# Order of the attention scores in layer 1, and of the passage from layer 0, in a four-layer graph kernel

## Chip, cores and metric

The kernel runs on one core of a Trainium2 chip. The metric is the device time of one execution in microseconds; lower is better. The engines of a core have instruction queues of their own and meet only at semaphores: PE (matrix products, which end in PSUM banks), DVE and ACT (elementwise work, reading PSUM and SBUF), POOL (elementwise work on SBUF), SP (issues DMA transfers here).

## What is computed

64 graphs of 128 nodes with 256 features pass four layers; each is followed by a residual and a layer norm, `x = layernorm(x + layer(x, adj))`. The change touches layer 0 at its end and layer 1. Layer 0 applies hypergraph convolution, relu, layer norm, hypergraph convolution. Layer 1 is, cut to its core:

```python
q, k = split(x @ W_qk.T)                # 64 columns each
v = x @ W_v.T
scores = (q @ k.T) / 8
w = sum(scores * adj, axis=-1)          # one number a node
w = softmax(w, over the nodes)
out = w * v
```

Since only the sum over the neighbours is needed, w(n) is q(n) times the sum of adj(n, m) k(m): one product of the adjacency matrix with k, then a row sum.

## The kernel before

Four graphs make a group; there are G = 16 groups. Each layer is written for each engine as a `step(g, p, has)`, which holds that engine's work of one step in a fixed order, for groups around g; `has(k)` is true when group g + k exists. `over_layers` runs all steps of one layer and then those of the next. At a passage between two layers a string (`SEAMS_ACT`, `SEAMS_POOL` and so on, one string a passage) says in which order the last steps of the old layer (o) and the first of the new one (n) are written. So the order on each engine is written by hand; no scheduler changes it.

Products are made in three float16 passes (`triple`, lines 86 to 88: low times high, high times low, high times high). For this every group of x is split into a high and a low half of float16 (tiles x_halves): ACT makes the high half (`x_high`, line 1123; for the first two groups of layer 1 `first_high`, line 720), POOL the low half (`x_low`, line 1130; `first_low`, line 967), and SP has both transposed by DMA (tiles xT_hi, xT_lo, line 1144; line 514 for the first two). Group g and g + 2 share one pair of buffers.

Layer 1, one step on each engine, in order:

- PE: `project(g - 1, 3)`, the fourth graph's product with W_qk and W_v of the group before (6 matmuls a graph); `weight_columns(g - 2)` (line 1236), which turns the softmax weights wn back to columns; `project(g, 0)`; `aggregate(g - 1)` (line 1224), adjacency times k, four graphs; `project(g, 1)` and one half of `project(g, 2)`; `score_rows(g - 1)` (line 1232), which turns the scores w to rows; the other half of `project(g, 2)`.
- ACT: `high_half(g + 3)`; `norms(g - 2)`, the four norm applies that write x_resident (line 1078); `copy_qkv(g + 1, 0)`, the first graph's v, q, k from PSUM to the tile l_vqk (line 1281); `exponentials(g)` (l_wexp, line 1293); the copies of graphs 1 to 3.
- DVE: the residuals l_pre of g - 2 (line 1327), `scores(g - 1)` (l_qa line 1341, l_w line 1348), two norm rows, `minimum(g - 1)` (l_wmin, line 1354), two norm rows, `softmax(g - 1)` (l_wrec line 1358, l_wn line 1362), and the norm's variance (ends in l_veps, line 1058).
- POOL: `norm_scales(g - 2)` (l_msum, l_mneg, l_rstd line 1069, l_nmr line 1072), then the low half of group g + 3.

Each engine runs on its own count of steps: the exponential of a group comes before its softmax, that before its weight columns, these before its residuals.

The end of layer 0: PE projects the hidden features h with W2 graph by graph (`project(g, j)`; graph j needs that zf of graph j - 2 is copied), ends with `square_sums` (line 616) and makes the last product in `mix_z` (line 629) out of zn. ACT copies zf (`copy_z`, line 702) and makes `squares_high` (hqs_hi, line 696); POOL adds the squares hq (line 973), makes `squares_low` (hqs_lo, line 980) and raises the variance to the power -1/2 (`hidden_power`, zrs, line 963); DVE makes zn (line 886), the low half of h (h_lo, line 839), and the counts rcs. In ACT's step G - 1 both `first_high` stand behind the last square of group G - 1 and ahead of the norm applies of G - 3 and of `copy_z(G - 1, 0)`. On POOL all of layer 0 is written before anything of layer 1.

Of the kernel before, what the change touches and what calls it, by code (L numbers as in the profile page):

```python
# [14 lines left out]
G = GRAPHS // GP  # L15
# [8 lines left out]
SEAMS_ACT = ('nnnonn', 'nononono', 'ooonnnonn')  # L24
SEAMS_DVE = ('oononn', 'onono', 'nonn')
SEAMS_POOL = ('ooooo', 'onno', 'ooonnn')
# [410 lines left out]
def layer0(nc, K, ctx, tiles, weights):  # L437
# [21 lines left out]
    L = norm(nc, ctx, "l0", 2, tiles)  # L459
# [209 lines left out]
    def scalar(act):  # L669
# [47 lines left out]
        def first_high(g):  # L717
            act.wait_ge(px_ps, upto(G - 2 + g, 2, 2))
            act.wait_ge(L.x_new, upto(g, GP, GP))
            act.activation(K.F.xs[g][0], x_group(K, g), ACT.Copy).then_inc(K.F.x_hi, 1)  # L720
# [8 lines left out]
        def step(g, p, has):  # L729
# [6 lines left out]
            if has(-1):  # L736
                copy_z(g - 1, 1)
                copy_z(g - 1, 2)
# [8 lines left out]
            if has(-1):  # L747
                copy_z(g - 1, 3)
            if has(0):
                hidden(g, 0)  # L750
                hidden(g, 1)
                square(g, 0)
# [14 lines left out]
            if isinstance(g, int) and g == G - 1:  # L767
                first_high(0)
                first_high(1)
            if has(-2):  # L770
                norm_apply(K, L, act, g - 2, p, 0)
                norm_apply(K, L, act, g - 2, p, 1)
                norm_apply(K, L, act, g - 2, p, 2)
                norm_apply(K, L, act, g - 2, p, 3)
            if has(0):
                copy_z(g, 0)
                squares_high(g)
# [171 lines left out]
    def gpsimd(pool):  # L949
# [32 lines left out]
        def step(g, p, has):  # L982
            q = 1 - p
            if isinstance(g, int) and g == G - 2:
                first_low(0)
                first_low(1)
# [4 lines left out]
            if has(0):  # L991
                norm_scales(K, L, pool, g, p)
            if has(1):
                hidden_power(g + 1)
            if has(2):
                sum_squares(g + 2, 1)
# [10 lines left out]
        return step, 2, 0  # L1007
# [140 lines left out]
def layer1(nc, K, ctx, tiles):  # L1148
# [41 lines left out]
    def tensor(pe):  # L1190
        def project(g, p, j, half=None):
            if j == 0:
                transposed(F, pe, g, p)
# [45 lines left out]
        def step(g, p, has):  # L1239
# [5 lines left out]
            if has(0):  # L1245
                project(g, p, 0)
            if has(-1) and g < G:
                aggregate(g - 1, q)
            if has(0):
                project(g, p, 1)  # L1250
                project(g, p, 2, 0)
            if has(-1) and g < G:
                score_rows(g - 1, q)
            if has(0):
                project(g, p, 2, 1)
# [10 lines left out]
    def scalar(act):  # L1266
# [29 lines left out]
        def step(g, p, has):  # L1296
# [5 lines left out]
            if has(1):  # L1302
                copy_qkv(g + 1, q, 0)
            if has(0) and g < G - 1:
                exponentials(g, p)
            if has(1):
                copy_qkv(g + 1, q, 1)
                copy_qkv(g + 1, q, 2)
# [761 lines left out]
```

## Time and profile before

| | |
|---|---|
| runs, median (lowest to highest) | 676.03 us (675.19 to 676.68), 3 runs |
| profiled execution | 676.46 us, span of its instructions 674.7 us |
| PE busy | 622.4 us, 92% of the span |
| DVE busy | 564.2 us, 84% |
| ACT busy | 525.5 us, 78% |
| POOL busy | 378.5 us, 56% |
| DMA | 76.14 MB, mean 113 GB/s |

Layer 0 lasts until about 290 us, layer 1 until about 387, layers 2 and 3 fill the rest. A busy share is a mean over all of it; what a reordering is worth is read from the stretches in which PE stands. A line of the timeline has the start, the duration, the engine, line and operation, the output and the inputs, and in square brackets the idle time of the engine ahead of it and what ended it. Durations of matmuls overlap.

### The profile page before, as it was taken

Reading aid. Unit: us, or ns where it says so; the run is one execution under the profiler, and the core shown is the slowest. Engines: PE = TensorE matmul, PEld = TensorE weight load, DVE = VectorE, ACT = ScalarE, POOL = GpSimd, SP = SyncE. Lnnn points to the kernel's source line nnn. Section 1 sums busy time; section 2 is a strip of 40 time slices with the busy share of each in tenths; the row PEclk is TensorE's granted clock in tenths of the full one; section 3 lists DMA queues with packets and bytes.
Section 4 is the critical chain, followed back from the end, with each engine's and each line's share of the span. In section 5 each row is a group of like instructions: output and inputs, shape, how many; then the busy total and the mean of one; then the engine's idle time right before and its main releaser. Section 6 shows DMA issues by size and latency. Waiting matters only on the chain.

```text
span 674.7 us, 15857 instructions
## 1 busy us (share of the span) xinstructions
PE 622.4 (92%) x5014; PEld 451.5 (67%) x5014; DVE 564.2 (84%) x1712; ACT 525.5 (78%) x1191; POOL 378.5 (56%) x448
## 2 busy tenths in 40 slices
PE   5889999999999999779999979999999996999993
PEld 4567777777777776556666647665766663788882
DVE  3889998888888886769999889898988987588886
ACT  4667888877777777767888777787877885799995
POOL 1335556665555555746777434443435353799983
PEclk9999999999999999989999999999999999999998
DMA  9781439464636322544665334445454443477883
GB/s 272 185 223 48 83 65 229 83 149 86 146 83 165 78 33 32 93 95 83 92 95 107 65 64 94 97 93 96 94 102 88 102 88 64 80 182 187 185 185 126
DMA packets 174467, 76.14 MB, mean 113 GB/s; under 512 B 122161, under 2 KB 173873, under 8 KB 174385
## 3 DMA queue, kind: packets, MB, share of 16 engines
q1 hardware_dynamic: 164208, 66.34, 42.9%
q0 software_dynamic: 8448, 8.39, 8.6%
q8 instruction: 41, 0.67, 0.4%
q10 hardware_dynamic: 1728, 0.40, 0.3%
q14 instruction: 42, 0.34, 0.2%
HBM read 28.97 MB, written 8.39 MB: 55 GB/s over the span
## 4 chain that ended last, share of the span: by engine, by line
PE 26%; POOL 9%; DVE 8%; ACT 6%; DMA 5%; issue 4%; ACTq 0%; POOLq 0%; SPq 0%; DVEq 0%
PE banks L86 8%; PE banks L88 8%; PE banks L87 8%; POOL l_rstd L1069 4%; DMA xT_lo<-x_halves 3%; ACT x_resident L1078 3%; POOL x_halves L1130 3%; DVE l_st L1044 2%; DMA l_TT_lo<-l_T_lo 2%; POOL l_U L2036 2%; PE banks L1593 1%; ACT l_wexp L1293 1%; DVE l_wn L1362 1%; DVE l_pre L2005 1%; DVE l_veps L1058 1%
## 5 line engine op out<-in xcount | busy, mean ns | idle before, releaser
L1078 ACT ACTIVATE x_resident<-l_pre,l_nmr,l_rstd 128x256 f32<-128x256 f32 x256 | 140.7, 605 | 15.6 <-POOL l_nmr L1072 15.6
L973 POOL TENSOR_TENSOR hq<-hq 128x512 f32<-128x512 f32 x48 | 69.5, 1448 | 93.7 <-ACT hq L690 91.4
L1130 POOL TENSOR_TENSOR x_halves<-x_resident,x_halves 128x1024 f16<-128x1024 f32 x46 | 98.1, 2134 | 3.9 <-ACT x_halves L1123 3.2
L1044 DVE BATCH_NORM_STATS2 l_st<-l_pre 128x6 f32<-128x256 f32 x256 | 93.4, 410 | 0.0
L86 PE MATMUL banks<-Wk_lo,xT_hi 128*128 128x512 f16 (+1 forms) x256 | 83.5, 326 | 3.2 <-DVE l_pre L1327 1.8
L1069 POOL TENSOR_TENSOR l_rstd<-l_veps,minus_half 128x4 f32<-128x4 f32 x64 | 74.9, 1170 | 17.9 <-DVE l_veps L1058 14.2
L87 PE MATMUL banks<-Wk_hi,xT_lo 128*128 128x512 f16 (+1 forms) x256 | 83.3, 325 | 0.0
L88 PE MATMUL banks<-Wk_hi,xT_hi 128*128 128x512 f16 (+1 forms) x256 | 83.2, 325 | 0.0
L86 PE MATMUL banks<-W2T_lo,h_hi 128*128 128x257 f16 x256 | 70.3, 274 | 5.3 <-ACT zf L702 4.4
L88 PE MATMUL banks<-W2T_hi,h_hi 128*128 128x257 f16 x256 | 70.1, 274 | 0.0
L87 PE MATMUL banks<-W2T_hi,h_lo 128*128 128x257 f16 x256 | 70.1, 274 | 0.0
L677 ACT ACTIVATE hf<-banks,b_col 128x512 f32<-128x512 f32 x64 | 44.5, 696 | 26.9 <-PE banks L88 26.8
L839 DVE TENSOR_TENSOR h_lo<-hf,h_hi 128x512 f16<-128x512 f32 x64 | 42.8, 690 | 12.1 <-issue 8.2
L1833 POOL TENSOR_TENSOR l_T_lo<-l_tf,l_T_hi 128x512 f16<-128x512 f32 x16 | 18.5, 1158 | 58.7 <-ACT l_T_hi L1684 58.7
L1063 POOL TENSOR_TENSOR l_msum<-l_st 128x4 f32<-128x4 f32 x64 | 13.6, 213 | 66.7 <-DVE l_st L1044 66.2
L86 PE MATMUL banks<-xT_lo,W1T_hi 128*128 128x512 f16 x128 | 48.6, 379 | 1.8 <-DVE xT_lo L853 1.1
L1123 ACT ACTIVATE x_halves<-x_resident 128x1024 f16<-128x1024 f32 x46 | 48.4, 1052 | 1.9 <-DMA xT_lo<-x_halves 1.9
L88 PE MATMUL banks<-xT_hi,W1T_hi 128*128 128x512 f16 x128 | 48.5, 379 | 0.0
L87 PE MATMUL banks<-xT_hi,W1T_lo 128*128 128x512 f16 x128 | 48.5, 379 | 0.0
L86 PE MATMUL banks<-w_lo,xT_hi 128*128 128x1 f16 (+1 forms) x256 | 45.5, 221 | 3.2 <-ACT l_xw L1934 1.9
L87 PE MATMUL banks<-w_hi,xT_lo 128*128 128x1 f16 (+1 forms) x256 | 46.5, 220 | 0.0
L88 PE MATMUL banks<-w_hi,xT_hi 128*128 128x1 f16 (+1 forms) x256 | 46.5, 221 | 0.0
(200 smaller groups left out, 1933.7 us busy)
## 6 DMA issues: line engine op xcount, KB each, us to landing
adj<-in_adj SPq DMA_DIRECT2D x32, 256.0 KB, 3.4
x_halves<-in_x SPq DMA_DIRECT2D x16, 512.0 KB, 4.4
x_resident<-b_half SPq DMA_DIRECT2D x8, 1024.0 KB, 7.1
x_resident<-in_x POOLq DMA_DIRECT2D x16, 512.0 KB, 6.0
out<-x_resident SPq DMA_DIRECT2D x15, 512.0 KB, 3.2
x_resident<-in_L_gnn_W SPq DMA_DIRECT2D x2, 512.0 KB, 5.5
x_resident<-in_L_gnn_Wk SPq DMA_DIRECT2D x1, 768.0 KB, 9.4
xT_hi<-x_halves SPq DMA_TRANSPOSE x48, 3.2
```

The source lines that it names most:

```text
L86: nc.tensor.matmul(out, lhs[0], rhs[1], start=start, stop=False, **kw)
L87: nc.tensor.matmul(out, lhs[1], rhs[0], start=False, stop=False, **kw)
L88: return nc.tensor.matmul(out, lhs[0], rhs[0], start=False, stop=stop, **kw)
L677: act.activation(hf[:, h, :], b_hid[h % 2][:], ACT.Relu, bias=K.b1[:, h:h + 1], scale=1.0 / W_SCALE).then_inc(hf_ok, 1)
L839: dve.tensor_tensor(hs[1][:, h, :], hf[:, h, :], hs[0][:, h, :], ALU.subtract).then_inc(h_lo, 1)
L973: pool.tensor_tensor(hq[:, 0, :], hq[:, 0, :], hq[:, h, :], ALU.add).then_inc(hqs_ok, 1)
L1044: dve.bn_stats(L.st[p][:, j, :], L.pre[p][:, j, :]).then_inc(L.st_ok, 1)
L1069: pool.tensor_tensor(L.rstd[p][:], L.veps[p][:], K.minus_half[:], ALU.pow).then_inc(L.rstd_ok, 1)
L1078: act.activation(K.x[:, gcols(g, j)], L.pre[p][:, j, :], ACT.Identity, bias=L.nmr[p][:, j:j + 1], scale=L.rstd[p][:, j:j + 1]).then_inc(L. ...
L1123: act.activation(F.xs[p][0], x_group(K, g), ACT.Copy).then_inc(F.x_hi, 1)
L1130: pool.tensor_tensor(F.xs[p][1], x_group(K, g), F.xs[p][0], ALU.subtract).then_inc(F.x_lo, 1)
L1833: pool.tensor_tensor(ts[1][:], tf[:], ts[0][:], ALU.subtract).then_inc(t_lo, 1)
```

## The change

It has two parts. In layer 1 PE makes `project(g, 0)` in two halves with `aggregate(g - 1)` between them, then `project(g, 1)`, then `score_rows(g - 1)`, then all of `project(g, 2)`; and ACT makes `exponentials(g)` ahead of `copy_qkv(g + 1, 0)`. At the passage from layer 0 the `first_high` move to ACT's steps G - 2 and G - 1, the `first_low` to POOL's steps G - 4 and G - 3, the zf copies of the last group are set between the norm applies of group G - 3, the last norm scales go behind `hidden_power` of the last group, and the low halves of groups 2 and 3 (layer 1) ahead of the norm scales of group G - 1.

```diff
 
 SEAMS_SP = ('noonnn', 'oono', 'onooonon')
 SEAMS_PE = ('nonn', 'onononono', 'oon')
-SEAMS_ACT = ('nnnonn', 'nononono', 'ooonnnonn')
+SEAMS_ACT = ('nnononn', 'nononono', 'ooonnnonn')
 SEAMS_DVE = ('oononn', 'onono', 'nonn')
-SEAMS_POOL = ('ooooo', 'onno', 'ooonnn')
+SEAMS_POOL = ('nonno', 'onno', 'ooonnn')
 
 W_SCALE = 64.0
 SQ_SCALE = 0.5
@@ -733,7 +733,7 @@
                 mixed_high(g, p, 1)
             once(g, -2, W.vectors, act)
             once(g, 0, W.high_w2, act)
-            if has(-1):
+            if has(-1) and g < G:
                 copy_z(g - 1, 1)
                 copy_z(g - 1, 2)
             once(g, 1, W.high_qkv, act)
@@ -744,8 +744,12 @@
             once(g, 4, W.high_w3, act)
             once(g, 5, W.high_wk, act, 0)
             once(g, 6, W.high_wk, act, 1)
-            if has(-1):
+            if g == G - 2:
+                first_high(0)
+            if has(-1) and g < G:
                 copy_z(g - 1, 3)
+            if g == G - 1:
+                first_high(1)
             if has(0):
                 hidden(g, 0)
                 hidden(g, 1)
@@ -764,15 +768,21 @@
             once(g, -1, W.halve_b2, act)
             if has(2):
                 copy_adj(g + 2)
-            if isinstance(g, int) and g == G - 1:
-                first_high(0)
-                first_high(1)
+            if g == G - 1:
+                copy_z(G - 1, 0)
             if has(-2):
                 norm_apply(K, L, act, g - 2, p, 0)
                 norm_apply(K, L, act, g - 2, p, 1)
+            if g == G - 1:
+                copy_z(G - 1, 1)
+            if has(-2):
                 norm_apply(K, L, act, g - 2, p, 2)
                 norm_apply(K, L, act, g - 2, p, 3)
-            if has(0):
+            if g == G - 1:
+                copy_z(G - 1, 2)
+                squares_high(G - 1)
+                copy_z(G - 1, 3)
+            if has(0) and g < G - 1:
                 copy_z(g, 0)
                 squares_high(g)
         return step, 2, 2
@@ -981,17 +991,20 @@
 
         def step(g, p, has):
             q = 1 - p
-            if isinstance(g, int) and g == G - 2:
-                first_low(0)
-                first_low(1)
             once(g, -2, W.constants, pool)
             once(g, -2, W.sum_rows, pool)
             if has(1):
                 squares_low(g + 1)
-            if has(0):
+            if has(0) and g < G - 2:
                 norm_scales(K, L, pool, g, p)
             if has(1):
                 hidden_power(g + 1)
+            if g > G - 2:
+                norm_scales(K, L, pool, g - 1, 1 - p)
+            if g == G - 4:
+                first_low(0)
+            if g == G - 3:
+                first_low(1)
             if has(2):
                 sum_squares(g + 2, 1)
             if has(0):
@@ -1004,7 +1017,7 @@
             once(g, 2, W.low_w3, pool)
             once(g, 3, W.low_wk, pool, 0)
             once(g, 4, W.low_wk, pool, 1)
-        return step, 2, 0
+        return step, 2, 1
 
     return sync, tensor, scalar, vector, gpsimd
 
@@ -1189,7 +1202,7 @@
 
     def tensor(pe):
         def project(g, p, j, half=None):
-            if j == 0:
+            if j == 0 and half != 1:
                 transposed(F, pe, g, p)
             if half == 1:
                 pass
@@ -1243,16 +1256,16 @@
             if has(-2) and g <= G:
                 weight_columns(g - 2, p)
             if has(0):
-                project(g, p, 0)
+                project(g, p, 0, 0)
             if has(-1) and g < G:
                 aggregate(g - 1, q)
             if has(0):
+                project(g, p, 0, 1)
                 project(g, p, 1)
-                project(g, p, 2, 0)
             if has(-1) and g < G:
                 score_rows(g - 1, q)
             if has(0):
-                project(g, p, 2, 1)
+                project(g, p, 2)
             if g == G + 1:
                 project(G - 1, 1, 3)
             if g == G + 2:
@@ -1299,11 +1312,10 @@
                 high_half(g + 3, q)
             if has(-2) and g < G - 1:
                 norms(g - 2, p)
-            if has(1):
-                copy_qkv(g + 1, q, 0)
             if has(0) and g < G - 1:
                 exponentials(g, p)
             if has(1):
+                copy_qkv(g + 1, q, 0)
                 copy_qkv(g + 1, q, 1)
                 copy_qkv(g + 1, q, 2)
             if has(1) and g < G - 2:
```

PE, one step in the steady part of layer 1, before (tiles named with their buffer numbers; l1_wn0 the weights of one group, l1_vqk1 the k of the next, xT0 the halves of the one behind it):

```order
L1236 MATMUL banks<-ident,l1_wn0 128x4
L86 MATMUL banks<-qkvT_lo,xT0_hi 128x384
L87 MATMUL banks<-qkvT_hi,xT0_lo 128x384
L88 MATMUL banks<-qkvT_hi,xT0_hi 128x384
L86 MATMUL banks<-qkvT_lo,xT0_hi 128x384
L87 MATMUL banks<-qkvT_hi,xT0_lo 128x384
L88 MATMUL banks<-qkvT_hi,xT0_hi 128x384
L1224 MATMUL banks<-l1_vqk1,adjT_resident 128x65 x4
```

and now:

```order
L1249 MATMUL banks<-ident,l1_wn0 128x4
L86 MATMUL banks<-qkvT_lo,xT0_hi 128x384
L87 MATMUL banks<-qkvT_hi,xT0_lo 128x384
L88 MATMUL banks<-qkvT_hi,xT0_hi 128x384
L1237 MATMUL banks<-l1_vqk1,adjT_resident 128x65 x4
L86 MATMUL banks<-qkvT_lo,xT0_hi 128x384
```

The adjacency products moved up by three matmuls; the matrix product that turns the scores to rows (with l1_w) now stands 12 matmuls behind the one with l1_wn0, not 15.

ACT, one step in the steady part of layer 1, before (x1_halves is the high half three groups on, l1_vqk1 v, q, k of one group, l1_wexp0 the exponential of the group before it):

```order
L1123 ACTIVATE x1_halves<-x_resident 128x1024
L1078 ACTIVATE x_resident<-l1_pre0,l1_nmr0,l1_rstd0 128x256 x4
L1281 ACTIVATE l1_vqk1<-banks 128x384
L1293 ACTIVATE l1_wexp0,l1_wsum0<-banks,l1_wmin0 4x128
L1281 ACTIVATE l1_vqk1<-banks 128x384 x3
L1123 ACTIVATE x0_halves<-x_resident 128x1024
```

and now:

```order
L1136 ACTIVATE x1_halves<-x_resident 128x1024
L1091 ACTIVATE x_resident<-l1_pre0,l1_nmr0,l1_rstd0 128x256 x4
L1306 ACTIVATE l1_wexp0,l1_wsum0<-banks,l1_wmin0 4x128
L1294 ACTIVATE l1_vqk1<-banks 128x384 x4
L1136 ACTIVATE x0_halves<-x_resident 128x1024
```

The exponential stands ahead of all four copies; the rest is as it was.

POOL, the end of layer 0, before, from the zrs of group G - 2 to that of G - 1 (x0_halves and x1_halves are the low halves of groups 0 and 1 of layer 1):

```order
L963 TENSOR_TENSOR zrs<-zvar,minus_half 128x4
L973 TENSOR_TENSOR hq<-hq 128x512
L952 DMA x_resident<-in_x 128x4x256
L973 TENSOR_TENSOR hq<-hq 128x512 x2
L967 TENSOR_TENSOR x0_halves<-x_resident,x0_halves 128x1024
L967 TENSOR_TENSOR x1_halves<-x_resident,x1_halves 128x1024
L980 TENSOR_TENSOR hqs_lo<-hq,hqs_hi 128x512
L1063 TENSOR_TENSOR l0_msum<-l0_st0 128x4
L1065 TENSOR_TENSOR l0_mneg<-l0_msum,minus_half 128x4
L1069 TENSOR_TENSOR l0_rstd0<-l0_veps0,minus_half 128x4
L1072 TENSOR_TENSOR l0_nmr0<-l0_mneg,l0_rstd0 128x4
L963 TENSOR_TENSOR zrs<-zvar,minus_half 128x4
```

and now, from the same zrs on:

```order
L973 TENSOR_TENSOR zrs<-zvar,minus_half 128x4
L977 TENSOR_TENSOR x1_halves<-x_resident,x1_halves 128x1024
L983 TENSOR_TENSOR hq<-hq 128x512
L962 DMA x_resident<-in_x 128x4x256
L983 TENSOR_TENSOR hq<-hq 128x512 x2
L990 TENSOR_TENSOR hqs_lo<-hq,hqs_hi 128x512
L973 TENSOR_TENSOR zrs<-zvar,minus_half 128x4
L1076 TENSOR_TENSOR l0_msum<-l0_st0 128x4
L1078 TENSOR_TENSOR l0_mneg<-l0_msum,minus_half 128x4
L1082 TENSOR_TENSOR l0_rstd0<-l0_veps0,minus_half 128x4
L1085 TENSOR_TENSOR l0_nmr0<-l0_mneg,l0_rstd0 128x4
L1143 TENSOR_TENSOR x0_halves<-x_resident,x0_halves 128x1024
```

The low half of group 0 went one step further up (behind the zrs of group G - 3), that of group 1 directly behind this zrs; the zrs of the last group stands ahead of the norm scales of group G - 2, and behind these follows the low half of group 2 (the last row), which stood behind the norm scales of group G - 1 before.

## Rows read from the trace of the kernel before

**Rows 1.** stages; columns: window, its length, busy (x count) by engine, PEclk, DMA share, GB/s

```profile
277.00:299.75 22.75, 14.95 (x106) 10.15 (x104) 17.23 (x36) 14.29 (x30) 15.33 (x16) 1.00 0.59 102
299.75:303.00 3.25, 3.25 (x13) 2.39 (x14) 0.00 (x0) 1.55 (x2) 2.02 (x1) 0.50 0.98 250
308.51:375.35 66.84, 64.34 (x424) 42.80 (x423) 60.69 (x217) 58.53 (x133) 49.28 (x61) 1.00 0.58 97
```

**Rows 2.** timeline of ACT, one period of layer 1

```profile
330.77 2.08 ACT L1078 ACTIVATE x_resident<-l_pre,l_nmr,l_rstd 128x256 f32<-128x256 f32 x4 [0.69 <-POOL l_nmr L1072]
332.75 0.47 ACT L1281 ACTIVATE l_vqk<-banks 128x384 f32<-128x384 f32 x1
333.12 0.34 ACT L1293 ACTIVATE l_wexp<-banks,l_wmin 4x128 f32<-4x128 f32 x1
...
333.46 1.21 ACT L1281 ACTIVATE l_vqk<-banks 128x384 f32<-128x384 f32 x3
...
336.34 2.08 ACT L1078 ACTIVATE x_resident<-l_pre,l_nmr,l_rstd 128x256 f32<-128x256 f32 x4 [0.72 <-POOL l_nmr L1072]
```

**Rows 3.** timeline of DVE, the same period

```profile
330.90 0.42 DVE L1341 SCALAR_TENSOR_TENSOR l_qa<-banks,l_vqk 128x256 f32<-128x256 f32 x1 [0.23 <-PE banks L1224]
...
332.48 0.28 DVE L1354 TENSOR_REDUCE l_wmin<-banks 4x1 f32<-4x128 f32 x1
...
333.59 0.15 DVE L1358 RECIPROCAL l_wrec<-l_wsum 4x1 f32<-4x1 f32 x1 [0.18 <-ACT l_wexp L1293]
...
334.56 1.69 DVE L1327 SCALAR_TENSOR_TENSOR l_pre<-l_vqk,banks,x_resident 128x256 f32<-128x256 f32 x4
```

**Rows 4.** timeline of POOL, the same period

```profile
334.62 1.29 POOL L1069 TENSOR_TENSOR l_rstd<-l_veps,minus_half 128x4 f32<-128x4 f32 x1 [0.61 <-DVE l_veps L1058]
...
336.32 2.13 POOL L1130 TENSOR_TENSOR x_halves<-x_resident,x_halves 128x1024 f16<-128x1024 f32 x1
```

**Rows 5.** timeline of PE, one period, four of its rows

```profile
334.14 0.38 PE L1236 MATMUL banks<-ident,l_wn 4*128 4x4 f32 x2 [0.24 <-DVE l_wn L1362]
...
335.44 1.00 PE L1224 MATMUL banks<-l_vqk,adjT_resident 128*128 128x65 f32 x8
336.27 0.33 PE L86 MATMUL banks<-qkvT_lo,xT_hi 128*128 128x384 f16 x1
...
337.74 0.27 PE L1232 MATMUL banks<-ident,l_w 128*4 128x128 f32 x1
```

**Rows 6.** timeline of PE, the passage from layer 0

```profile
280.22 0.28 PE L86 MATMUL banks<-W2T_lo,h_hi 128*128 128x257 f16 x1 [2.55 <-ACT zf L702]
...
284.30 0.16 PE L616 MATMUL banks<-ones,hqs_lo 128*128 128x1 f16 x1 [1.25 <-issue]
...
299.75 0.50 PE L86 MATMUL banks<-qkvT_lo,xT_hi 128*128 128x384 f16 x1 [3.55 <-DMA xT_lo<-x_halves]
```

**Rows 7.** timeline of POOL, the passage

```profile
278.87 4.21 POOL L967 TENSOR_TENSOR x_halves<-x_resident,x_halves 128x1024 f16<-128x1024 f32 x2
...
293.57 4.21 POOL L1130 TENSOR_TENSOR x_halves<-x_resident,x_halves 128x1024 f16<-128x1024 f32 x2
```

**Rows 8.** chain of waits, the passage: start, us, what

```profile
295.72 3.99 DMA xT_lo<-x_halves
```

**Rows 9.** timeline of DVE, the passage

```profile
269.38 1.67 DVE L886 SCALAR_TENSOR_TENSOR zn<-zf,zrs,W2beta_rows 128x256 f32<-128x256 f32 x4 [1.13 <-POOL zrs L963]
...
294.94 0.83 DVE L1362 TENSOR_SCALAR l_wn<-l_wexp,l_wrec 4x128 f32<-4x128 f32 x1
296.24 3.01 DVE L1327 SCALAR_TENSOR_TENSOR l_pre<-l_vqk,banks,x_resident 128x256 f32<-128x256 f32 x4 [0.47 <-PE banks L1236]
```

**Rows 10.** timeline of ACT, end of layer 0 and first norm apply of layer 1

```profile
251.17 0.39 ACT L702 ACTIVATE zf<-banks 128x257 f32<-128x257 f32 x1 [1.31 <-PE banks L88]
...
268.76 0.69 ACT L677 ACTIVATE hf<-banks,b_col 128x512 f32<-128x512 f32 x1 [1.11 <-PE banks L88]
...
308.51 2.08 ACT L1078 ACTIVATE x_resident<-l_pre,l_nmr,l_rstd 128x256 f32<-128x256 f32 x4 [0.67 <-POOL l_nmr L1072]
```

## Prediction

> **What bounds the kernel now.** I read the page first, then the windows by stage, then the timeline of each engine over one period of layer 1, and last the timeline of the passage from layer 0. The page gives PE 92% of the span, so a change that only reorders work can win only where PE stands still or waits in a loop with the others. Two such places lie where the change works.
>
> *Layer 1 in its steady part.* From 308.51 to 375.35 us layer 1 takes twelve equal periods of 5.57 us; a twelfth of the busy times is PE 5.36, DVE 5.06, ACT 4.88 us, at granted clock 1.00 [rows 1]. None is full, so I looked for a loop. It is there in the rows, with starts counted from x_resident on ACT at 330.77: the four norm applies until the copy at 332.75 (1.98), that copy (0.37), the exponential until the reciprocal on DVE at 333.59 (0.47), wn and the variance until rstd on POOL at 334.62 (1.03), rstd and nmr until the next x_resident at 336.34 (1.72) [rows 2 to 4]. The sum is 5.57, the whole period. PE waits in it: 0.24 us ahead of the weight columns at 334.14 [rows 5]. The matmul ends are modelled: one lasts 0.33 but the next starts 0.163 later (nine between 336.27 and 337.74 [rows 5]), so PE is really free some 0.17 earlier and needs 5.57 - 0.41 = 5.16 us a period. DVE waits 0.23 (for the adjacency products) and 0.18 (for the exponential) [rows 3]: it needs 5.16 too.
>
> *The passage.* Between 277.00 and 299.75 PE is busy 14.95 of 22.75 us [rows 1]. Its three large waits: 2.55 us for zf, which ACT copies only after two x_halves and four norm applies; 1.25 us for the squares, which stand on POOL behind 4.21 us of x_halves; 3.55 us for the transposed halves of group 2 [rows 6, 7]. Those came late because POOL made x_halves at 293.57, behind norm scales, and the transposition followed at 295.72 and took 3.99 [rows 7, 8]. After that wait PE runs 3.25 us at granted clock 0.50, the 1.2 GHz level, where it was 1.00, the 2.4 GHz level, before the wait [rows 1]; the 2.55 us wait didn't bring it down.
>
> **The change, steady part.** No instruction is added or dropped in the period. On ACT the exponential moves ahead of the first copy of v,q,k, so the copy's 0.37 us leaves the loop: 5.57 - 0.37 = 5.20. The copy itself costs nothing there: its reader is PE's project(g+2, 0) behind the weight columns, 0.5 us or more away, and the fourth copy keeps its place since the two only change places. The condition is that the minimum is ready at 332.75. It ends at 332.48 + 0.28 = 332.76 [rows 3], a tie; the PE edit makes room: the products come three matmuls earlier (3 x 0.163 = 0.49 us), of which DVE can use its 0.23 us wait, and the turned scores come 12 matmuls behind the weight columns and not 15, so they are not late for the minimum.
>
> The PE edit has a price. The products wait for the fourth copy, which ends at 333.46 + 1.21 = 334.67; they start at 335.44 [rows 2, 5], 0.77 later. Now they come 0.49 earlier by order and up to 0.37 earlier with wn: 0.09 too early, and with some 0.15 from release to first matmul they start 0.2 to 0.25 later than PE could. Following it round: products at x_resident + 4.10; 5.16 - 0.31 - 0.49 = 4.36 on, the weight columns; 0.42 on, l_pre; 1.68 on, qa; 1.58 on, the minimum, which ends 2.02 behind the next x_resident (ready 2.08), against 1.98 wanted. That adds up to 0.1 to one round, and settled over several rounds the period is 5.25 us; bounds 5.20 (the ACT loop alone) and 5.57 (nothing gained). A loss has no row for it except the rival below. I take 5.25, since every term but the 0.15 is read: 12 x 0.32 = **3.8 us gained**.
>
> **The change, passage.** *Price.* The first two low halves on POOL (4.21 us for two [rows 7]) move two and one steps up, each right behind zrs. For the second the rows show what stands beside it: the same zrs releases DVE's zn x4 at 269.38 [rows 9]. While POOL works on x_halves (from 293.57, two of 2.1 us [rows 7]) some DVE operations wait: wn at 294.94 lasts 0.83 and ends at 295.77, as the first of the two ends, and l_pre x4, begun at 296.24 inside the second, takes 3.01 against 1.69 in the steady part [rows 3, 9]. zn, too, has two inputs in SBUF. So zn comes 2.1 us later. PE's mix_z waits 0.9 for it, and the fourth h_lo behind it is late for the W2 projection: 1.0 to 1.1 us lost. One step up the same happens to rcs_lo and zn: 1.1 more. Together 2.1; bounds 0 and 4.2. The high halves on ACT (about 1.0 us each) fall into its waits for PE of 1.31 us ahead of zf and 1.11 ahead of hf [rows 10], and cost nothing; without that cover it would be 1.0 each.
> The Trainium skill (SBUF — State Buffer, "SBUF: two separate sides") says that POOL and a DVE operation with two SBUF inputs share one pair of ports and the first holds it for its whole instruction; by that rule the trace agrees for x_halves.
>
> *Gain.* ACT copies zf(0) right after the last squares, so the 2.55 goes; POOL goes to the squares' low half without the 4.21, and its next limit is ACT's high half behind the third zf copy. Counted with the 2.1 of shift: last W2 projections end 282.4, square sums 283.3 instead of 284.30. zrs now stands ahead of the norm scales: zn at 285.2, mix_z at 286.5, 1.1 earlier. Then POOL makes the low half of group 2 at 287.1 to 289.2 (now 293.57), SP issues its transposition right behind the high one, at 290.7 instead of 295.72, landing at 294.7. PE is then held by wn of group 0: ACT reaches that exponential at 293.0 (norm apply waits for the fourth copy now), and wn runs into the low half of group 3 on POOL, until 295.1. project(2) starts at 295.7 instead of 299.75, at full clock. One period on, wn of group 1 runs into the low half of group 4 (POOL 300.1 to 302.3), so weight columns at 302.6, rstd 303.0, first x_resident of the steady part at **304.7 instead of 308.51** [rows 10]: **3.8 us gained**, the price already in it. Bounds: 1.7 if the two stalls cost all of 4.2, 7.5 if neither they nor the wn collisions come (2.1 + 1.6 more).
>
> Behind layer 1 nothing is touched; the shift is carried on, since PE, DVE and ACT go on in order. Adjacency loads for layer 2 stand long before their use.
>
> **The sum** is made against the profiled execution's 676.46 us (span 674.7): 676.46 - 3.8 - 3.8 = 668.9. The median of the runs is 0.43 lower, 676.03; so 668.4.
>
> **Rivals.** (a) *The loop gains nothing.* PE, waiting for the fourth copy, is late with the weight columns, and DVE with the minimum, by as much as ACT wins. For it: three engines need 5.16 to 5.20, a tie. Against: 0.25 us of wait is less than the 0.41 PE has. Time 676.0 - 3.8 = 672.2.
> (b) *The passage gains nothing.* The port stalls in layer 0 and the two at wn eat it. For: four stalls of up to 2.1 us. Against: 3.55 us and the half clock behind it fall away. Time 676.0 - 3.8 = 672.2.
> (c) *Slower: POOL takes the ports ahead of the fourth l_pre in each period.* Now l_pre x4 starts at 334.56, its fourth at 335.8, and x_halves on POOL at 336.32 [rows 3, 4]: 0.5 us of room. It decides from there: if the weight columns are more than 0.5 late behind wn, the fourth l_pre waits 2.1 us, and with it products, minimum and exponential: some 1.8 a period. The period behind it, PE is early again, so I count every second: 6 x 1.8 = 11 lost against 7.6 gained, 679.4; every period would be 690. Against it: I find PE 0.1 to 0.2 late, not 0.5.
> The same page's rule would have rstd, if it started first, hold the ports for its whole time and push l_pre back 1.0 us, which is this rival; the rows show rstd at 334.62 running 1.29 us beside an unbroken l_pre x4 of 1.69 [rows 3, 4], so I give it little.
> (d) *Both gains fail*: the order moves but the waits come back elsewhere; 676.0.
>
> **Chances.** Forecast 0.60, (a) 0.14, (b) 0.12, (c) 0.08, (d) 0.06. The forecast's own range is 665.5 to 671.5: period 5.20 to 5.35, passage 2.3 to 5.5. The range to 673.5 takes in (a) and (b). A measurement of this kernel can tell about 0.2%, 1.35 us: faster 0.86, same 0.04, slower 0.10 ((c) and a third of (d)).
>
> **What would show it.** Steady part: x_resident groups 5.25 us apart; the exponential right behind the fourth norm apply; on PE the wait ahead of the weight columns gone or under 0.1 and a new small one, 0.1 to 0.3, ahead of the products, released by l_vqk. l_pre x4 still 1.69 long (3.8 would be rival (c)). Passage: no 2.55 wait for zf; zn or the operations ahead of it stretched to about 2 us at two places near 253 and 270; mix_z waiting some 0.9 us there; wn stretched near 294 and 301; no stretch of clock 0.50 near 300; first l1 x_resident near 304.7. The forecast is wrong if POOL isn't the one that gets the ports at zrs (then more is gained), or if the period stays at 5.5.

## The result and the profile after

The changed kernel takes 669.38 us, the median of 4 runs (667.3 to 671.4); the kernel before 675.61 (675.01 to 676.68), 6.2 us more. The ratio on record, worked out from the runs, is 0.9875, 95% interval 0.984 to 0.9909: 6 to 11 us faster. It is not the quotient of these two medians, which is 0.9908, at the slow edge of that interval; a repeat below gave 0.9883. The forecast was 668.4. The profiled execution lies at 670.04 with a span of 668.2; PE is busy 623.1 us of it, 93%.

The steady part of layer 1 first. Windows of the changed kernel; columns as in [rows 1]:

```profile
305.00:309.00 4.00, 4.00 (x16) 2.00 (x15) 2.86 (x11) 2.96 (x8) 2.55 (x3) 0.57 0.14 26
311.00:366.00 55.00, 55.00 (x370) 37.21 (x369) 49.82 (x189) 52.01 (x115) 38.58 (x52) 1.00 0.58 104
```

In the second line PE is busy 55.00 of 55.00 us; in the kernel before it was 64.34 of 66.84 [rows 1]. The loop is gone and PE bounds the stage. One period, of ACT, DVE, POOL and PE in this order, to hold beside [rows 2 to 5]:

```profile
332.59 2.07 ACT L1091 ACTIVATE x_resident<-l_pre,l_nmr,l_rstd 128x256 f32<-128x256 f32 x4
334.92 0.36 ACT L1306 ACTIVATE l_wexp<-banks,l_wmin 4x128 f32<-4x128 f32 x1 [0.26 <-DVE l_wmin L1366]
...
331.56 1.69 DVE L1339 SCALAR_TENSOR_TENSOR l_pre<-l_vqk,banks,x_resident 128x256 f32<-128x256 f32 x4 [0.45 <-PE banks L1249]
...
331.20 1.01 POOL L1082 TENSOR_TENSOR l_rstd<-l_veps,minus_half 128x4 f32<-128x4 f32 x1 [0.36 <-DVE l_veps L1071]
333.33 2.13 POOL L1143 TENSOR_TENSOR x_halves<-x_resident,x_halves 128x1024 f16<-128x1024 f32 x1 [0.79 <-DVE l_pre L1339]
...
331.15 0.38 PE L1249 MATMUL banks<-ident,l_wn 4*128 4x4 f32 x2
336.41 0.38 PE L1249 MATMUL banks<-ident,l_wn 4*128 4x4 f32 x2
```

The weight columns follow each other 5.26 us apart and PE waits for nothing ahead of them, where it waited 0.24 [rows 5]. x_resident no longer waits (0.69 [rows 2]); the exponential waits 0.26 for the minimum, and l_pre 0.45 for PE. The small wait ahead of the products that I had forecast isn't there. Last, rstd takes 1.01 where it took 1.29 [rows 4]: it now starts ahead of l_pre, not behind it.

The passage: PE's 2.55 us wait for zf and its wait for the transposed halves [rows 6] are gone, others stand there. Rows of PE, DVE and POOL:

```profile
284.18 0.16 PE L616 MATMUL banks<-ones,hqs_lo 128*128 128x1 f16 x1 [0.94 <-issue]
295.94 0.38 PE L1249 MATMUL banks<-ident,l_wn 4*128 4x4 f32 x2 [0.56 <-ACT l_vqk L1294]
303.15 0.38 PE L1249 MATMUL banks<-ident,l_wn 4*128 4x4 f32 x2 [1.87 <-DVE l_wn L1374]
...
254.37 1.98 DVE L818 TENSOR_TENSOR rcs_lo<-rcnt,rcs_hi 128x4 f16<-128x4 f32 x1
271.68 3.53 DVE L896 SCALAR_TENSOR_TENSOR zn<-zf,zrs,W2beta_rows 128x256 f32<-128x256 f32 x4 [1.12 <-POOL zrs L973]
301.32 1.77 DVE L1374 TENSOR_SCALAR l_wn<-l_wexp,l_wrec 4x128 f32<-4x128 f32 x1
...
254.20 2.13 POOL L977 TENSOR_TENSOR x_halves<-x_resident,x_halves 128x1024 f16<-128x1024 f32 x1
271.62 2.11 POOL L977 TENSOR_TENSOR x_halves<-x_resident,x_halves 128x1024 f16<-128x1024 f32 x1
300.90 2.12 POOL L1143 TENSOR_TENSOR x_halves<-x_resident,x_halves 128x1024 f16<-128x1024 f32 x1 [3.19 <-issue]
```

The two stalls in layer 0 are rcs_lo and zn, each beside a low half on POOL; the long wait is for wn, stretched by the low half that began 0.42 us ahead of it. From 305.13, 2 us behind the end of this wait, PE ran 3.4 us at granted clock 0.50, the 1.2 GHz level (the window from 305 above shows 0.57).

Executions start layer 1 up to 3.7 us apart for reasons outside the change, so I count from one instruction that all kernels have, the single zf copy at 251.17 [rows 10] (252.15 in the changed kernel). "first x_resident" is that of the steady part, at 308.51 before [rows 10]; "14th" is the start of the 14th weight columns of layer 1, at 372.79 before; "gained" is against before, there.

| kernel | zf mark | first x_resident | 2nd weight columns | 14th | gained |
|---|---|---|---|---|---|
| before | 251.17 | 57.34 | 55.14 | 121.62 | |
| changed | 252.15 | 53.20 | 51.00 | 115.84 | 5.78 |
| layer 1 alone | 252.27 | 56.65 | 55.21 | 119.88 | 1.74 |
| passage alone | 250.39 | 53.21 | 51.01 | 117.50 | 4.12 |
| PE edit alone | 250.29 | 57.57 | 56.13 | 120.87 | 0.75 |
| ACT edit alone | 252.57 | 57.96 | 55.75 | 119.56 | 2.06 |
| changed again | 253.94 | 53.20 | 51.00 | 114.35 | 7.27 |
| exponential first | 253.82 | 53.54 | 49.06 | 114.69 | 6.93 |
| scales first too | 252.38 | 51.29 | 49.05 | 114.11 | 7.51 |
| zeroed low halves | 252.22 | 51.60 | 49.40 | 114.41 | 7.21 |
| lighter, before | 251.06 | 57.40 | 55.20 | 121.42 | 0.20 |
| lighter, changed | 253.74 | 53.20 | 51.00 | 112.70 | 8.92 |
| low halves late | 251.03 | 55.94 | 53.74 | 119.23 | 2.39 |

### The profile page after: what moved, and what is told of

The parts are those of the page before. It is cut to its first block, busy times and chain, and to the rows that moved or that the text cites. A ratio compares the mean times of both kernels' runs of the same rounds, so it can differ in the third digit from the quotient of the medians.

```text
span 668.2 us, 15857 instructions
## 1 busy us (share of the span) xinstructions
PE 623.1 (93%) x5014; PEld 452.0 (68%) x5014; DVE 560.8 (84%) x1712; ACT 526.6 (79%) x1191; POOL 376.5 (56%) x448
## 4 chain that ended last, share of the span: by engine, by line
PE 30%; DVE 8%; POOL 6%; DMA 6%; ACT 3%; issue 2%; SPq 0%; ACTq 0%; POOLq 0%; DVEq 0%
PE banks L86 9%; PE banks L88 8%; PE banks L87 8%; DMA xT_lo<-x_halves 3%; DMA l_TT_lo<-l_T_lo 3%; DVE l_st L1057 2%; POOL x_halves L1143 2%; POOL l_rstd L1082 2%; PE banks L1237 2%; POOL l_U L2048 1%; PE banks L1605 1%; POOL l_T_lo L1845 1%; ACT l_t L1658 1%; DVE l_u L1762 1%; DVE l_rsum L1768 1%
## 5 line engine op out<-in xcount | busy, mean ns | idle before, releaser
L983 POOL TENSOR_TENSOR hq<-hq 128x512 f32<-128x512 f32 x48 | 71.7, 1493 | 90.9 <-ACT hq L690 88.6
L1082 POOL TENSOR_TENSOR l_rstd<-l_veps,minus_half 128x4 f32<-128x4 f32 x64 | 71.7, 1121 | 15.1 <-DVE l_veps L1071 11.2
L681 ACT ACTIVATE h_hi<-banks,b_col 128x512 f16<-128x512 f32 x64 | 44.4, 694 | 0.0
```

The lines of the kernel that those rows point to most:

```text
L681: act.activation(hs[0][:, h, :], b_hid[h % 2][:], ACT.Relu, bias=K.b1[:, h:h + 1], scale=1.0 / W_SCALE).then_inc(h_hi, 1)
L983: pool.tensor_tensor(hq[:, 0, :], hq[:, 0, :], hq[:, h, :], ALU.add).then_inc(hqs_ok, 1)
L1082: pool.tensor_tensor(L.rstd[p][:], L.veps[p][:], K.minus_half[:], ALU.pow).then_inc(L.rstd_ok, 1)
```

## Experiments

Each kernel ran beside the kernel before on its chip; ratios are to that.

**Each half alone, and each edit of the first half alone.** The layer 1 half is the hunks of the diff in layer 1's `tensor` and `scalar`; its PE edit and its ACT edit were also made alone:

```diff
                 project(g, p, 0, 0)
             if has(-1) and g < G:
                 aggregate(g - 1, q)
             if has(0):
+                project(g, p, 0, 1)
                 project(g, p, 1)
-                project(g, p, 2, 0)
```

```diff
-            if has(1):
-                copy_qkv(g + 1, q, 0)
             if has(0) and g < G - 1:
                 exponentials(g, p)
             if has(1):
+                copy_qkv(g + 1, q, 0)
```

> Only the two edits inside layer 1 (adjacency products between the halves of the first projection, scores turned behind the second, exponential ahead of the first copy); the passage as before. Theory: the loop over ACT is opened and PE becomes the bound, period 5.26 us as in the changed kernel, 12 periods x 0.31 = 3.7 us faster than before (ratio 0.9945), 0.2 us idle ahead of the weight columns gone. Rival: part of the gain came with the passage (layer 1 entered in another phase): period 5.4 or more, under 2 us faster.

> Only the other order at the passage; layer 1 inside as before. Theory: first norm apply of layer 1 some 4.1 us earlier relative to layer 0, of which a stretch of PE at granted clock 0.50 behind the wait for wn of group 1 takes back 1.7, period 5.57: 2.4 us faster (ratio 0.9965). Rival one: no half clock in this order, then 4.1 faster. Rival two: the stalls of DVE in layer 0 eat it, within 1 us of before.

> Only PE's order in layer 1 is changed; ACT and the passage as before. Theory: the loop of norm apply, first copy, exponential, softmax, variance, rstd is untouched, so the period stays 5.57 us and the time within 0.5 us of before. Rival: the earlier adjacency products are what opens the loop: period 5.3 to 5.4, 2 to 3 us faster.

> Only ACT's order in layer 1 is changed (exponential ahead of the first copy); PE and the passage as before. Theory: the loop loses 0.37 us, but the minimum is ready only 0.1 us behind the wanted place and DVE still waits 0.2 for the products: period 5.35 to 5.40, 2.0 to 2.6 us faster. Rival: the PE edit adds nothing, period 5.26, 3.7 faster.

Measured: layer 1 alone 674.1 us, 0.9963 (0.9945 to 0.9982); passage alone 672.84, 0.9944 (0.9925 to 0.9964); PE edit alone 673.68, 0.9952 (0.9931 to 0.9972); ACT edit alone 673.83, 0.996 (0.9941 to 0.9979).

The passage's trace gives the very 53.2 of the changed kernel for the first x_resident, and then the old period: its 12 intervals from the 2nd to the 14th weight columns last 5.32 to 5.58. No stretch of clock 0.50 follows there. So the two halves are separate, as forecast.

The whole run of the passage alone, 3.8 us less (2.4 to 5.1), lies near the rival of its expectation, 4.1 without a half clock; the 2.4 of the theory is at the edge of the interval, and the trace, which has no such stretch, goes with the rival.

The two single edits are the surprise. I had expected nothing of PE's alone and part of the gain of ACT's, and either alone brings the whole period: the weight columns come 5.26 apart with the PE edit and 5.27 with the ACT edit. PE's rows and POOL's and DVE's for one period of the kernel with the PE edit alone:

```profile
333.60 0.38 PE L1236 MATMUL banks<-ident,l_wn 4*128 4x4 f32 x2
338.86 0.38 PE L1236 MATMUL banks<-ident,l_wn 4*128 4x4 f32 x2
...
333.65 1.01 POOL L1069 TENSOR_TENSOR l_rstd<-l_veps,minus_half 128x4 f32<-128x4 f32 x1 [0.32 <-DVE l_veps L1058]
...
334.01 1.69 DVE L1327 SCALAR_TENSOR_TENSOR l_pre<-l_vqk,banks,x_resident 128x256 f32<-128x256 f32 x4 [0.45 <-PE banks L1236]
```

Here the copy is still in the loop, but another 0.33 us has left it. In the kernel before l_pre started at 334.56 and rstd at 334.62, and from rstd to the next x_resident it took 1.72 us [rows 2 to 4]. Here rstd starts 0.36 ahead of l_pre, lasts 1.01, and x_resident starts at 335.04, 1.39 behind it. The loop is 5.57 - 0.33 = 5.24, and PE's 5.26 stands above it. With the ACT edit alone l_pre keeps its place ahead of rstd, as these rows of DVE and POOL show:

```profile
335.10 1.69 DVE L1326 SCALAR_TENSOR_TENSOR l_pre<-l_vqk,banks,x_resident 128x256 f32<-128x256 f32 x4
...
335.18 1.28 POOL L1069 TENSOR_TENSOR l_rstd<-l_veps,minus_half 128x4 f32<-128x4 f32 x1 [0.33 <-DVE l_veps L1058]
```

There the copy's 0.37 has left the loop and nothing else; the loop is 5.27 by its rows, and PE no longer waits either, a tie. With both, PE is the only bound, so the second edit adds nothing here.

That the single edits show 0.75 and 2.06 us at the 14th weight columns has two other causes: transposed low halves that land late (below), which the layer 1 half shares, and in these two executions alone a longer stretch of clock 0.50 around the 3.55 us wait of [rows 6]. With the PE edit alone, in the columns of [rows 1]:

```profile
298.00:304.00 6.00, 5.12 (x20) 3.41 (x21) 1.91 (x6) 1.55 (x2) 2.12 (x1) 0.50 0.71 156
```

In the kernel before the stretch lasted 3.4 us, from 299.66 to 303.07, most of it the second window of [rows 1]; here it lasted 6.8, from 297.4 to 304.2, and the second weight columns came 1.0 later than before.

**What the loop gives when PE has room.** In both kernels the product of x's high half with the low half of the weights was left out for groups 4 to 15 of layer 1.

```diff
-                    m = triple(nc, b_qkv[j][:, 0:2 * QK + D], [s[:, j, d, :] for s in F.xT[p]],
-                               [w[:, d, :] for w in K.qkv], start=d == 0, stop=d == DT - 1)
+                    m = (pair if 4 <= g < G else triple)(
+                        nc, b_qkv[j][:, 0:2 * QK + D], [s[:, j, d, :] for s in F.xT[p]],
+                        [w[:, d, :] for w in K.qkv], start=d == 0, stop=d == DT - 1)
```

> The kernel before, and in layer 1 the projections of groups 4 to 15 without their product of x's high half with the low half of the weights: 8 of 32 matmuls and more a group, 8 x 0.163 = 1.3 us of PE a period, are left out of the computation. It asks what bounds the steady part. Theory: the loop through ACT, DVE and POOL does, PE only waits in it, so the period stays at 5.57 us and the time at that of before (within 1 us). Rival: PE is part of what makes the period, and it falls to 5.3 or less: 3 us or more faster.

> The changed kernel with the same matmuls left out. Its PE is full at a period of 5.26 us; now PE needs 3.96. Theory: the loop that is left takes over at once. Counted from x_resident: norm applies 2.0, exponential to reciprocal 0.5, wn and variance to rstd 1.0, and rstd, nmr to the next x_resident 1.72, if rstd (1.29) runs beside l_pre, which now starts right behind wn since PE is early: 5.2 to 5.3 us, so leaving out a quarter of PE's work gains under 1 us. Rival: rstd stays at 1.01 and its stretch at 1.39: then 4.9 to 5.0, and 3.5 us or more faster than the changed kernel.

Measured: 677.48 us, ratio 1.001 (0.9984 to 1.0037), and 668.0, ratio 0.987 (0.9826 to 0.9913). The theory held in both; that the second gains under 1 us on the changed kernel (0.9883 in the repeat below) rests on intervals that overlap, and in its trace the 14th weight columns come 1.65 earlier than in the repeat's. Weight columns, of the lighter kernel before and of the lighter changed one:

```profile
328.43 0.38 PE L1242 MATMUL banks<-ident,l_wn 4*128 4x4 f32 x2 [1.34 <-DVE l_wn L1368]
333.96 0.38 PE L1242 MATMUL banks<-ident,l_wn 4*128 4x4 f32 x2 [1.34 <-DVE l_wn L1368]
```

```profile
325.19 0.38 PE L1255 MATMUL banks<-ident,l_wn 4*128 4x4 f32 x2 [0.56 <-DVE l_wn L1380]
330.38 0.38 PE L1255 MATMUL banks<-ident,l_wn 4*128 4x4 f32 x2 [0.59 <-DVE l_wn L1380]
```

Before, a quarter of PE's work in the period buys no time: the columns come 5.53 apart, and of the 1.3 us 1.1 come back as wait for wn (1.34, where it was 0.24 [rows 5]). In the changed kernel the period falls from 5.26 to 5.19, just under the 5.2 to 5.3 expected, and a new loop takes over. POOL, DVE and ACT there:

```profile
336.04 1.28 POOL L1087 TENSOR_TENSOR l_rstd<-l_veps,minus_half 128x4 f32<-128x4 f32 x1 [0.62 <-DVE l_veps L1076]
...
335.96 1.69 DVE L1345 SCALAR_TENSOR_TENSOR l_pre<-l_vqk,banks,x_resident 128x256 f32<-128x256 f32 x4
...
337.74 2.08 ACT L1096 ACTIVATE x_resident<-l_pre,l_nmr,l_rstd 128x256 f32<-128x256 f32 x4 [0.32 <-POOL l_nmr L1090]
```

With PE early, l_pre (335.96) is ahead of rstd again, which lasts 1.28 and not 1.01, and x_resident waits again, 1.70 behind rstd's start. That is the loop of 5.20 that the prediction worked out.

**The changed kernel again, and the wait for wn.** On another chip, the changed kernel itself beside three others. In the second the exponential of group 1 goes ahead of the high half of group 4, in the third also the norm scales of group 0 ahead of the low half of group 4:

```diff
+            if g == 1:
+                exponentials(g, p)
             if halves_due(F, g + 3):
                 high_half(g + 3, q)
```

```diff
                 norm_scales(K, L, pool, g - 2, p)
-            if halves_due(F, g + 3):
+            if g == 2:
+                low_half(4, 0)
+            if halves_due(F, g + 3) and g != 1:
                 low_half(g + 3, 1 - p)
```

> The changed kernel as it is, on the same chip as the three kernels beside it. Theory: the two halves of the change add up. Layer 1 alone gave 0.9963 and the passage alone 0.9944, so both give 0.9963 x 0.9944 = 0.9907, 6.3 us less than before (5.0 to 7.6). Rival: the two help each other beyond that, because a passage that ends earlier also leaves layer 1 without the late transposed halves that layer 1 alone showed (waits of 0.8 and 0.6 us): then 0.9875 as measured first, 8.4 us less.

> The changed kernel, with the exponential of group 1 put ahead of the high half of group 4 on ACT, once, at the passage; all else stays. Theory: PE's 1.87 us wait for wn of group 1 (at 301.28) comes from wn running beside POOL's low half and lasting 1.77; now wn ends before that low half begins, PE waits under 0.3 us, no stretch of granted clock 0.50 follows, and the next weight columns come 0.6 us earlier by the order and up to 1.4 more without the half clock: 1 to 2 us faster than the changed kernel beside it. Rival: l_pre of group 1, three inputs of which two lie in SBUF, now meets the low half in place of wn and lasts 3.7 instead of 1.69; the products wait for nothing of it, but the next exponential does, and nothing is gained (0 to 0.5).

> As the kernel with the exponential of group 1 first, and on POOL the norm scales of group 0 of layer 1 ahead of the low half of group 4. Theory: rstd starts near 301.4 instead of 303.7 and x_resident of group 0 near 302.9 instead of 305.35, counted in the time of the changed kernel's trace; the low half runs 302.8 to 305 and its transposed copy lands near 308, 1.5 us behind the end of project(3), so PE trades its wait for wn for one of 1 to 1.5 us for the transposed halves: the same time as the kernel with only the exponential moved, within 0.7 us. Rival: the transposed half lands in time and 1.5 us more are gained.

Measured: 668.88 us, ratio 0.9883 (0.986 to 0.9907); 667.84, 0.9867 (0.9848 to 0.9885); 668.97, 0.988 (0.9863 to 0.9898). The changed kernel lies between the product of its halves (0.9907, the edge of the interval) and the first measurement. Moving the exponential removes the 1.88 us wait and brings the second weight columns 1.94 earlier, but the third come at 56.51 behind the mark against 56.27 in the changed kernel beside it: nothing is left. The low half on POOL (from 302.91) now meets l_pre in place of wn, and PE waits for what it delays:

```profile
303.30 3.22 DVE L1341 SCALAR_TENSOR_TENSOR l_pre<-l_vqk,banks,x_resident 128x256 f32<-128x256 f32 x4 [0.45 <-PE banks L1249]
...
304.32 1.10 PE L1237 MATMUL banks<-l_vqk,adjT_resident 128*128 128x65 f32 x8 [0.37 <-ACT l_vqk L1294]
307.36 0.27 PE L1245 MATMUL banks<-ident,l_w 128*4 128x128 f32 x1 [0.48 <-DVE l_w L1362]
310.33 0.38 PE L1249 MATMUL banks<-ident,l_wn 4*128 4x4 f32 x2 [0.74 <-DVE l_wn L1376]
```

By its trace the rival of that kernel was right (l_pre 3.22 long, 3.7 forecast); its whole run, 1.0 us less by the medians, would suit the lower edge of the theory too, but the intervals overlap and can't decide. In the third PE never waits for the transposed halves, as I had forecast; it waits 0.82 for l_w, behind an l_pre of 3.57 beside the same low half, and its 14th weight columns come 0.6 earlier than in the second. By their times neither of the two can be told from the changed kernel.

**What the first two low halves cost and bring.** In one kernel POOL sets them to zero in place of the subtraction, so that it reads no SBUF; in the other they stand at their old place, the rest as changed:

```diff
-            pool.tensor_tensor(K.F.xs[g][1], x_group(K, g), K.F.xs[g][0], ALU.subtract).then_inc(K.F.x_lo, 1)
+            pool.memset(K.F.xs[g][1], 0.0).then_inc(K.F.x_lo, 1)
```

```diff
+            if g == G - 2:
+                first_low(0)
+                first_low(1)
...
-            if g == G - 4:
-                first_low(0)
-            if g == G - 3:
-                first_low(1)
```

> The changed kernel with the low halves of groups 0 and 1 set to zero by POOL in place of the subtraction of two SBUF tensors; this leaves out the low part of x in two groups. Theory: the subtraction takes the ports from rcs_lo and zn at 254 and 271.7 (1.98 in place of 0.16 us, 3.53 in place of 1.67). Without it the hidden copy that came 17.43 us behind its mark comes 16.1 behind it, PE's waits for mix_z and h_lo (0.25, 0.96, 0.32, 0.34) go, and the time falls by 1.3 us. Rival: the later waits, for zf, squares and wn, take the gain up, since ACT and POOL set them: under 0.4 us.

> The changed kernel with the first two low halves back at their old place on POOL, behind layer 0's last but one hidden power, all else as changed. It asks what of the passage's gain hangs on them. Theory: the port stalls in layer 0 go (1.6 us by the kernel with zeroed halves), but the squares' low half stands behind 4.2 us of low halves again, so the square sums come 31.6 us behind the hidden copy that I count from, as before, and not 30.5: 1.1 us later than the changed kernel, all of it carried on: ratio to before 0.990, first x_resident of layer 1 at 52.8 instead of 51.7. Rival: the squares have room once ACT copies zf early, and the kernel is 1 us or more faster than the changed one.

Measured: 668.38 us, 0.9883 (0.9863 to 0.9904); and 672.59, 0.9927 (0.99 to 0.9955). With zeroed halves the first x_resident comes at 51.60 and not 53.20: the stalls cost 1.60 us in the passage. (Zeroing also takes POOL 0.94 us in place of 2.1, so its own time is in this.) The whole run shows nothing of the 1.3 us expected: 668.38 against 668.88. In its profiled run a stretch of clock 0.50 behind the wait for wn took the gain back: from the second to the third weight columns it needs 6.89 where the changed kernel, without such a stretch, needed 5.27.

With the halves late the stalls go too, yet the kernel is slower than the changed one, by 3.0 us if the ratio is set beside that of the repeat. These two intervals just touch (0.99 and 0.9907); the traces say the same more clearly, the 14th weight columns come 3.4 us later than in the first profiled execution of the changed kernel and 4.9 later than in the second. The first x_resident comes 2.74 later, not 1.1. The square sums stand at 33.10 behind the mark, where I had put them (31.6 behind a copy 1.50 later), 1.07 later than in the changed kernel. What I had missed is what PE does behind this wait, now 3.96 us long. PE's rows, and ACT's for the buffer that I suspected first:

```profile
284.13 0.16 PE L616 MATMUL banks<-ones,hqs_lo 128*128 128x1 f16 x1 [3.96 <-issue]
...
285.30 0.33 PE L86 MATMUL banks<-qkvT_lo,xT_hi 128*128 128x384 f16 x1
...
285.74 0.53 PE L88 MATMUL banks<-qkvT_hi,xT_hi 128*128 128x384 f16 x1
286.06 0.53 PE L86 MATMUL banks<-qkvT_lo,xT_hi 128*128 128x384 f16 x1
...
288.93 1.89 PE L629 MATMUL banks<-zn,P 128*128 128x256 f32 x8
...
284.12 1.06 ACT L1135 ACTIVATE x_halves<-x_resident 128x1024 f16<-128x1024 f32 x1 [3.54 <-DMA xT_lo<-x_halves]
285.50 0.49 ACT L1293 ACTIVATE l_vqk<-banks 128x384 f32<-128x384 f32 x1 [0.32 <-PE banks L88]
```

and the same mix_z in the changed kernel, where the clock stayed at 1.00:

```profile
287.31 1.89 PE L629 MATMUL banks<-zn,P 128*128 128x256 f32 x8
```

From 285.51 to 288.92 the granted clock was 0.50 and the matmuls followed each other 0.32 apart in place of 0.163. From the square sums to mix_z PE needed 4.80 us, in the changed kernel 3.13: 1.67 more. With the 1.07 that is the 2.74. Group 2's high half, which goes to the buffer of group 0 and waits 3.54 us for its transposition, is not on this path: ACT is through with it and waits for PE again at 285.50.

## Why the prediction came out right, and where its steps did not

**The loop is what bounded the kernel before: shown.** The sum of 5.57 from [rows 2 to 4] stood, and a quarter less PE work moved nothing.

**The period, 5.25 forecast, 5.26 measured, for part of a wrong reason.** I had PE at 5.16 and a small wait ahead of the products. PE in fact needs 5.26 with no wait at all: the step that failed is "PE is really free some 0.17 earlier", which took the idle of 0.24 and the overlap of 0.17 both off the period. Only some 0.3 of the two could be used. The wait that I then added to reach 5.25 isn't there: that the two errors cancelled was luck. The gain was 12 x 0.32 by the sum. Measured from the second to the 14th weight columns it is 66.48 - 63.35 = 3.1 us in the second profiled execution of the changed kernel, which had no stretch of clock 0.50 there; the mean period before was 5.54, not 5.57.

**Which edit does it: missed.** I gave the ACT edit the gain and the PE edit the part of a helper. Each alone is enough. The step that failed was to take rstd's stretch of 1.72 as fixed in the loop; it is 1.39 when l_pre starts behind rstd, and PE decides that. I had both rows in [rows 3, 4], 0.06 us apart, and read no term from them. The ACT edit did what I said, taking the copy's 0.37 out, but PE needs 5.26, so 0.06 of it had no use.

**The passage, 3.8 forecast, 4.14 measured** (57.34 less 53.20). The price was 1.6 by the zeroed halves, not 2.1; the square sums came at 32.03 behind the mark instead of 33.13. Most of the gain lies further on: from the first to the second weight columns it took 10.49 us before and 7.21 now, 3.28 less, where the 3.55 us wait for group 2's halves and the stretch of clock 0.50 at it stood. The kernel with the late low halves has this part too (7.20). Their early place, which I had counted as a price with a gain on POOL, carries 2.7 of the 4.1 us there, 1.07 by the order and 1.67 by the clock behind the longer wait, of which I said nothing. I had 3.8 in each part; 3.1 and 4.14 add up to 7.3 against 7.6, so here, too, two errors of opposite sign help the total.

**"No stretch of clock 0.50 near 300": wrong in the profiled run.** wn stretched as forecast (1.44 and 1.77), PE waited 1.87 us for it, and the clock fell 2 us later: the third weight columns came at 57.94 against 56.27 in the second profiled execution, which has the same wait and no fall. Of these 1.67 us 1.5 were left at the 14th, which is why the gain there is 5.78 and not 7.3. Windows of that second execution, between the same weight columns:

```profile
304.94:310.21 5.27, 5.26 (x36) 3.55 (x36) 4.95 (x21) 3.45 (x10) 4.28 (x7) 1.00 0.41 76
```

and of the first:

```profile
303.15:310.09 6.94, 6.94 (x35) 4.13 (x35) 5.23 (x22) 4.05 (x10) 4.72 (x8) 0.75 0.31 58
```

**Rival (c), slower, had no chance, and not for my reason.** I let the order on the ports decide. But POOL's low half waits for the fourth l_pre of group g - 4 by a semaphore: in the changed kernel it waits 0.79 us for l_pre at 333.33. What starts behind l_pre by construction can't get in ahead of it. The code had said so.

**rstd ahead of l_pre.** The trace shows rstd at 331.20 and l_pre starting 0.36 us later inside it, unbroken at 1.69. The rows that I had held against this rival had l_pre first, and so did not test it. The Trainium skill (SBUF — State Buffer, "SBUF: two separate sides") would have l_pre held until rstd ends; for this operation of 128x4 the runs say no, as far as the spans on POOL can be trusted, which are rough; for the low half of 128x1024 they say yes.

**What stays open.** The layer 1 half alone gained 1.74 at the 14th weight columns, not 3.1, because two low halves were transposed late. PE in that kernel:

```profile
319.17 0.34 PE L86 MATMUL banks<-qkvT_lo,xT_hi 128*128 128x384 f16 x1 [0.78 <-DMA xT_lo<-x_halves]
356.67 0.34 PE L86 MATMUL banks<-qkvT_lo,xT_hi 128*128 128x384 f16 x1 [0.59 <-DMA xT_lo<-x_halves]
```

The first was issued at 314.19, 4.98 us ahead of its use; the median from issue to landing is 3.2. At a period of 5.57 no trace has such a wait, though the passage alone had a transfer of 4.8 us; at 5.26 it shows. The profiled execution of the changed kernel has none that late (in layer 1 its longest is 4.1, against 4.6 before). Why they come where they do wasn't found. Nor was the passage taken apart further: the zf copies, the high halves and the order around zrs were only run together, so which of them removes the 3.55 us wait is argued from the rows and not shown.

## To carry to other kernels

Write the loop between the engines as a sum and look for every term that depends on which of two instructions starts first: a tie of 0.06 us between l_pre and rstd held a third of a microsecond a period. The PE edit tipped it; the ACT edit left it and took another third of a microsecond out. When a stage leaves a loop for a bound of one engine, further edits to the loop buy nothing; a version with a quarter of that engine's work left out shows what is behind it. A wait of PE can cost more than its length, because the matmuls behind it may run at half the clock (1.07 us of order became 2.74 here); price it with and without. And when a wait looks like the cause, see what the engine waits for next: ACT's 3.54 us for a buffer ended in one more wait for PE.

## What the runs showed of the hardware

- A POOL subtraction of 128x1024 (two in a row in the last line below) also holds up DVE operations that read little: l_wn (4x128 and a scalar a partition) lasted 1.44 and 1.77 in place of 0.28, rcs_lo (128x4) 1.98, and in the kernel with late low halves two operations of 128x4 in a row:

```profile
278.80 2.05 DVE L1066 SCALAR_TENSOR_TENSOR l_dd<-l_mdiff 128x4 f32<-128x4 f32 x1
280.89 2.04 DVE L1070 SCALAR_TENSOR_TENSOR l_veps<-l_m,l_dd 128x4 f32<-128x4 f32 x1
...
278.70 4.21 POOL L977 TENSOR_TENSOR x_halves<-x_resident,x_halves 128x1024 f16<-128x1024 f32 x2
```

- The granted clock doesn't follow from the length of a wait alone. At the wait of 3.55 us it fell to 0.50 in all five profiled executions that have it (in three of them before the wait had ended), behind that of 3.96 in the one that has it, behind that of 2.54 in three of five, behind that of 1.87 in three of six (the changed kernel fell in one execution and not in the other). Where PE was the bound, a fall cost 1.6 to 1.7 us up to the next weight columns or mix_z; behind the wait of 2.54 it cost nothing, the first weight columns come 44.65 behind the mark in all five.
